# One-hot lookups of a DLRM tower: two tables in one 512-column VectorE instruction, one id buffer per pair, first loads in another order

## What is computed

```
all_vecs = concatenate([dense_proj[:, None, :], sparse_embs], axis=1)      # 2048 x 27 x 128
interactions = einsum('bnd,bmd->bnm', all_vecs, all_vecs)
z = concatenate([dense_proj, interactions[:, rows, cols]], axis=1)         # upper triangle, 351
h = maximum(concatenate([z, dense]) @ W_top1 + b_top1, 0)                  # 607 -> 512
h = maximum(h @ W_top2 + b_top2, 0)                                        # 512 -> 256
y = h @ W_top3                                                             # 256 -> 1
```

## Time and profile before

| | |
|---|---|
| median of 3 runs | 370.9 us |
| the profiled execution, whole | 370.56 us |
| its span, first to last instruction | 368.6 us |
| TensorE busy (products) | 338.4 us, 92% |
| VectorE busy | 241.6 us, 66% |
| ScalarE busy | 140.9 us, 38% |
| GpSimd busy | 245.3 us, 67% |
| DMA | 36.90 MB, mean 100 GB/s |

### The profile page before, as it was taken

How to read it: one execution, slowest core, us unless ns; L and a number is a source line. 1 busy time by engine, 2 the same in 40 slices (tenths; PEclk the granted TensorE clock), 3 DMA queues, 4 the chain that set the end, 5 groups by cost and what they waited for, 6 DMA issues and landing times.

```text
span 368.6 us, 14267 instructions
## 1 busy us (share of the span) xinstructions
PE 338.4 (92%) x6096; PEld 309.5 (84%) x6096; DVE 241.6 (66%) x702; ACT 140.9 (38%) x232; POOL 245.3 (67%) x260
## 2 busy tenths in 40 slices
PE   0686689999999999999999999999999999999797
PEld 0585589999899898989899998989999998998675
DVE  4999999998565856578565974677664884601300
ACT  2246432535143541344343441444442450447132
POOL 5777777777777777777777777777767777760000
PEclk9989999999999999999999999999999999999999
DMA  6999944332244212611243111521244112220000
GB/s 192 284 245 245 290 140 124 79 106 54 58 152 123 59 50 67 205 56 52 55 145 125 50 51 50 188 83 50 52 140 129 50 50 55 73 57 4 18 2 0
DMA packets 16567, 36.90 MB, mean 100 GB/s; under 512 B 5462, under 2 KB 8542, under 8 KB 16544
## 3 DMA queue, kind: packets, MB, share of 16 engines
q1 hardware_dynamic: 8335, 19.77, 18.0%
q0 software_dynamic: 8192, 16.79, 17.6%
q10 hardware_dynamic: 16, 0.01, 0.0%
HBM read 36.54 MB, written 0.01 MB: 99 GB/s over the span
## 4 chain that ended last, share of the span: by engine, by line
PE 85%; DVE 7%; issue 3%; DMA 3%; POOL 2%; ACT 0%; DVEq 0%
PE hid L387 14%; PE gram L413 13%; PE look_ps L341 8%; PE vec_act L314 7%; PE look_ps L343 7%; PE look_odd L341 7%; PE look_odd L343 7%; PE hid L394 7%; DVE onehot L557 5%; PE hid L341 4%; PE hid L343 4%; DMA vecs<-tbl,ids_sb 2%; DVE look_lo L565 2%; POOL vecs L297 2%; PE small L356 1%
## 5 line engine op out<-in xcount | busy, mean ns | idle before, releaser
L297 POOL DMA_INDIRECT vecs<-tbl,ids_sb x256 | 245.1, 957 | 85.1 <-issue 75.9
L557 DVE TENSOR_SCALAR onehot<-step_ids,row_no 125x256 fp32r<-125x256 int32 x640 | 199.0, 381 | 74.6 <-PE look_odd L343 35.0
L532 ACT COPY vecs_T<-vec_act 128x512 f32<-128x512 f32 x64 | 46.3, 732 | 102.2 <-PE vec_act L314 102.2
L341 PE MATMUL look_odd<-onehot,look_hi 125*128 125x256 f32 x256 | 67.3, 300 | 4.6 <-DVE look_lo L565 4.6
L341 PE MATMUL look_ps<-onehot,look_hi 125*128 125x256 f32 x256 | 67.8, 301 | 2.3 <-DVE look_lo L565 2.3
L343 PE MATMUL look_ps<-onehot,look_lo 125*128 125x256 f32 x256 | 63.7, 284 | 0.0
L343 PE MATMUL look_odd<-onehot,look_lo 125*128 125x256 f32 x256 | 62.9, 283 | 0.0
L413 PE MATMUL gram<-vecs_T 128*27 128x26 f32 x4096 | 52.8, 192 | 5.9 <-issue 3.3
L413 PEld LDWEIGHTS gram<-vecs_T 128*27 128x27 f32 x4096 | 44.1, 104 | 15.0 <-issue 9.1
L341 PEld LDWEIGHTS look_odd<-onehot,look_hi 125*128 125x128 f32 x256 | 48.8, 191 | 5.5 <-DVE look_lo L565 5.2
L341 PEld LDWEIGHTS look_ps<-onehot,look_hi 125*128 125x128 f32 x256 | 49.2, 192 | 3.2 <-DVE look_lo L565 2.7
(11 more groups left out here) (70 smaller groups left out, 282.2 us busy)
## 6 DMA issues: line engine op xcount, KB each, us to landing
step_ids<-look_ids SPq DMA_DIRECT2D x15, 640.0 KB, 4.5
raw<-tbl SPq DMA_DIRECT2D x10, 448.0 KB
vecs<-tbl,ids_sb POOLq DMA_INDIRECT x256
dense_new<-dense SPq DMA_DIRECT2D x8, 128.0 KB
dense_T<-dense SPq DMA_DIRECT2D x8, 128.0 KB, 2.9
raw<-tbl SPq DMA_DIRECT2D x10, 52.0 KB
step_ids<-look_ids SPq DMA_DIRECT2D x1, 512.0 KB
w_sb<-w SPq DMA_DIRECT2D x1, 512.0 KB
```

Source lines behind the costliest of these rows:

```text
L297: nc.gpsimd.indirect_dma_start(out=vecs[j][:, k, :], out_offset=None, in_=tables[k], in_offset=bass.IndirectOffsetOnAxis(ap=ids_sb[:, t, k ...
L341: nc.tensor.matmul(bank, look_hi[:, f, ch, :], onehot[:, i % SLOTS, c, :], start=ch == 0, stop=False)
L532: return engine_copy(vecs_T[j][:, :, lo:lo + GROUP], bank[:, :, :].rearrange("d v b -> d b v"))
L557: last = nc.vector.tensor_scalar(onehot[:, i % SLOTS, c, :], step_ids[a][0:LOOK_K, f - a * LOOKUPS // 2, :], row_no[0:LOOK_K, ch:ch + 1], ...
```

## The change

A unit becomes a quarter of a duo: 2 chunks of both tables. VectorE makes a chunk for two tables with one `tensor_scalar` of 125x512, so 2 instructions for a unit; TensorE still has 8 products of 256 columns to a unit, now alternating between the two halves of the bank. Only the first product of a bank carries `start`. A pair still has 20 units and the ring still five slots of the same size.

In the loading stage TensorE has an order of its own, `look_up_first`: all four units of a duo for its first table, then all four for its second, and only in the second round does it count `onehot_used` up. VectorE makes the first unit of a duo ahead of the last `take_low` of the duo before. The ids of a pair lie in one buffer `pair_ids`, loaded in two pieces (four tables, six tables), in pair 0 in four. The transposes of tile 0 now come after duos 0 and 1 and after duo 3.

```diff
-UNIT_CH = LOOK_CH // 2
+UNIT_CH = LOOK_CH // 4
+DUO_UNITS = LOOK_CH // UNIT_CH
+PIECES = ((0, 4), (4, LOOKUPS))
-        step_ids = [sb(f"step_ids{a}", [P, STEP_IDS, PAIR], I32) for a in range(2)]
-        onehot = sb("onehot", [LOOK_K, SLOTS, UNIT_CH, PAIR], F32R)
+        pair_ids = sb("pair_ids", [P, LOOKUPS, PAIR], I32)
+        onehot = sb("onehot", [LOOK_K, SLOTS, UNIT_CH, 2 * PAIR], F32R)
-        FIRST_TURN, SECOND_TURN = 4, 4
+        FIRST_TURN, SECOND_TURN = 2, 4
...
+                def load_ids(pair, tables, loaded):
+                    lo, hi = tables
+                    if positive(pair):
+                        sp.wait_ge(onehot_made, 2 * STEP_UNITS * (pair - 1) + hi * DUO_UNITS // 2)
...
-                load_step(0, 0, 0, slice(0, 1), first_ids_in)
+                load_ids(0, (0, 2), first_ids_in)
                 load_table(0)
-                load_step(0, 0, 0, slice(1, STEP_IDS))
                 load_table(1)
+                load_ids(0, (2, 4), pair_ids_in[0])
                 sp.dma_start(ident[:, :], identity).then_inc(ident_in, 16)
+                load_table(2)
                 load_dense_new(0)
-                load_table(2)
-                load_step(1, 1, 0)
                 load_table(3)
-                for f in range(4, LOOKUPS):
+                load_ids(0, (4, 6), middle_ids_in)
+                load_table(4)
+                load_table(5)
+                load_ids(0, (6, LOOKUPS), pair_ids_in[1])
+                for f in range(6, LOOKUPS):
                     load_table(f)
                 load_dense(0)
-                load_step(2, 0, 1)
+                load_ids(1, PIECES[0], pair_ids_in[0])
...
-                load_step(3, 1, 1)
+                load_ids(1, PIECES[1], pair_ids_in[1])
                 load_dense_new(1)
                 with sp.Fori(2, pairs) as r:
-                    load_step(2 * r, 0, r)
-                    load_step(2 * r + 1, 1, r)
+                    load_ids(r, PIECES[0], pair_ids_in[0])
+                    load_ids(r, PIECES[1], pair_ids_in[1])
...
+                def look_chunk(duo, v, part, c, slot):
+                    ch = part * UNIT_CH + c
+                    cols = slice(v * PAIR, (v + 1) * PAIR)
+                    bank = look_ps[DUO_BANK[duo]][:, cols]
+                    nc.tensor.matmul(bank, look_hi[:, 2 * duo + v, ch, :], onehot[:, slot, c, cols],
+                                     start=ch == 0 and v == 0, stop=False)
+                    return nc.tensor.matmul(bank, look_lo[:, 2 * duo + v, ch, :], onehot[:, slot, c, cols],
+                                            start=False, stop=ch == LOOK_CH - 1 and v == 1)
...
+                    for c in range(UNIT_CH):
+                        for v in range(2):
+                            last = look_chunk(duo, v, part, c, i % SLOTS)
                     last.then_inc(onehot_used, 1)
+                def look_up_first(duo):
+                    wait_for_bank(0, duo)
+                    for v in range(2):
+                        pe.wait_ge(table_split, 2 * duo + v + 1)
+                        for part in range(DUO_UNITS):
+                            n = duo * DUO_UNITS + part
+                            if v == 0:
+                                pe.wait_ge(onehot_made, n + 1)
+                            for c in range(UNIT_CH):
+                                last = look_chunk(duo, v, part, c, n % SLOTS)
+                            if v == 1:
+                                last.then_inc(onehot_used, 1)
...
+                for duo in range(DUOS):
+                    if duo == FIRST_TURN:
                         pe.wait_ge(ident_in, 16)
                         turn_half(0, 0, 0, 0)
-                for i in range(LOOKUPS):
-                    if i == SECOND_TURN:
+                    if duo == SECOND_TURN:
                         turn_half(0, 0, 0, 1)
-                    look_up(1, 1, 0, i)
+                    look_up_first(duo)
...
-                for s in range(2):
-                    for i, f, half in units(s):
-                        if i == 2 * (1 - s):
-                            dve.wait_ge(step_ids_in[s], 16)
-                        make_unit(s, s, i, f, half)
-                        if half == 1:
-                            take_low(f)
+                make_unit(0, *units(0)[0])
+                for duo in range(DUOS):
+                    for n in range(duo * DUO_UNITS + 1, (duo + 1) * DUO_UNITS):
+                        make_unit(n // STEP_UNITS, *units(n // STEP_UNITS)[n % STEP_UNITS])
+                    take_low(2 * duo)
+                    n = (duo + 1) * DUO_UNITS
+                    if duo == 0:
+                        dve.wait_ge(pair_ids_in[0], 16)
+                    if duo == 1:
+                        dve.wait_ge(middle_ids_in, 16)
+                    if duo == 2:
+                        dve.wait_ge(pair_ids_in[1], 16)
+                    if duo < DUOS - 1:
+                        make_unit(n // STEP_UNITS, *units(n // STEP_UNITS)[n % STEP_UNITS])
+                    take_low(2 * duo + 1)
...
+                for f in range(4):
+                    take_high(f)
+                take_first(0)
+                take_high(4)
+                for q in range(HALF_GROUPS):
+                    copy(0, 0, q)
+                place_dense(0, 0, 0)
+                take_high(5)
+                take_first(1)
+                take_high(6)
+                take_high(7)
+                take_first(2)
+                take_high(8)
+                take_first(3)
+                for q in range(HALF_GROUPS, GROUPS):
+                    copy(0, 0, q)
+                take_high(9)
+                take_first(4)
```

More of the change, by code:

```diff
@@ L51 @@
 SLOTS = 5
-HALF_UNITS = LOOKUPS // 2
+STEP_UNITS = LOOKUPS
+HALF_UNITS = STEP_UNITS // 2
 GATHERS = TABLES - LOOKUPS
@@ new lines, in wait_for_bank @@
+                def wait_for_bank(pair, duo):
+                    if positive(DUOS * pair + duo + 1 - DUO_BACK[duo]):
+                        pe.wait_ge(looked_up, DUOS * pair + duo + 1 - DUO_BACK[duo])
+                    if duo == 0 and positive(pair - 2):
+                        pe.wait_ge(h2_copied, pair - 1)
+                def look_chunk(duo, v, part, c, slot):
[6 more added lines that the diff above has]
+                                            start=False, stop=ch == LOOK_CH - 1 and v == 1)
@@ new lines, in look_up @@
+                def look_up(s, a, pair, i):
+                    _, duo, part = units(a)[i]
+                    pe.wait_ge(onehot_made, STEP_UNITS * s + i + 1)
+                    if part == 0:
+                        wait_for_bank(pair, duo)
+                    for c in range(UNIT_CH):
+                        for v in range(2):
+                            last = look_chunk(duo, v, part, c, i % SLOTS)
+                    last.then_inc(onehot_used, 1)
+                def look_up_first(duo):
[10 more added lines that the diff above has]
+                                last.then_inc(onehot_used, 1)
@@ L574, in unit @@
                         if look:
-                            make_unit(t + 2, j, *made[i])
-                    if look:
-                        dve.wait_ge(step_ids_in[j], 16 * (pair + 2))
+                            if j == 0 and made[i][2] == 0 and made[i][1] in (0, PIECES[1][0] // 2):
+                                dve.wait_ge(pair_ids_in[made[i][1] > 0], 16 * (pair + 2))
+                            make_unit(t + 2, *made[i])
                     for i in range(HALF_UNITS):
@@ L734, in _, with take_first @@
                 act.sem_inc(y_copied, 1)
-                ahead = LOOKUPS // 2
-                for k in range(ahead):
-                    take_high(k)
-                for s in range(2):
-                    for i, f, half in units(s):
-                        if s == 0 and i == FIRST_TURN:
-                            for q in range(HALF_GROUPS):
-                                copy(0, 0, q)
-                            place_dense(0, 0, 0)
-                        if s == 1 and i == SECOND_TURN:
-                            for q in range(HALF_GROUPS, GROUPS):
-                                copy(0, 0, q)
-                        take_looked(s, s, 0, i)
-                        if half == 1 and f + ahead < LOOKUPS:
-                            take_high(f + ahead)
+                def take_first(duo):
+                    n = (duo + 1) * DUO_UNITS - 1
+                    take_looked(n // STEP_UNITS, n // STEP_UNITS, 0, n % STEP_UNITS)
+                for f in range(4):
[16 more added lines that the diff above has]
+                take_first(4)
                 tile(0, 0, 0, first=True, mlp=False)
```

58 lines of the change are left out of this document (18 added, 40 removed).

## The result

The changed kernel takes 380.9 us (median of 4 runs; 378.26 to 384.37), the kernel before beside it 371.0 (370.31 to 371.51). The run of 384.37 us is a slow one and is left out of the ratio, which is 1.0245, 95% interval 1.0188 to 1.0302. The forecast was 374.2, with a range up to 376.2. The direction was right, but by luck: the stage that was to lose 2.5 us gained 3.4, and the loss came from work that the forecast had priced at nothing. The medians differ by 9.9 us. The profiled execution is the shortest of the four, 378.26 us with a span of 376.4 against 368.6, so the traces can explain 7.8 us.

What follows compares the result with a forecast made beforehand. The prediction took TensorE, 92% busy, as the bound, so only its end of the loading stage counted: 370.56 + 2.5 (later end of that stage) + 1.1 (one clock fall) = 374.2 us, range 370.9 to 376.2.

Steps and rivals of the forecast that it cites:

- the stage that was to lose 2.5 us: Loading stage, start of the run: TensorE was to end it at 49.05 instead of 46.56, +2.5 us.
- One-hot: 0.58 from start to start: VectorE's 512-column one-hot: 0.58 us each, a unit 1.16 instead of 1.28, 2.4 us less on VectorE in the loading stage.
- the five cases: Forecast with zero to two clock falls 0.78; gap closes 0.07; ring not binding 0.08; one-hot twice as fast 0.03; slower products or late ids 0.04.
- rival 4: Wide one-hot twice as fast, 0.32 us; TensorE ends the loading stage some 5 us earlier, 365.6 us; chance 0.03.
- The ring: Loading stage: VectorE waits for a free unit slot, losing 0.91 us a duo; a duo takes 7.93 us instead of 7.49.
- my own formula: Length of a duo in the loading stage: 2.10 + 3 x 1.16 + 1.19 + 1.16 = 7.93 us.
- the schedule: Timetable of the loading stage: VectorE starts at 6.2 instead of 5.71, TensorE is done at 49.05, +2.5 us.
- Everything behind is TensorE's own work and moves along: After the loading stage: only TensorE's end of that stage counts; later distances stay, steady part changes by at most 1 us.
- I priced POOL at nothing: GpSimd's gathers, whole run: no term in the sum; no engine but TensorE was above 67% busy.
- The clock: TensorE idle 3.5 us after tables 1 and 5 in the loading stage: one fall to half clock, +1.1 us.
- rival 2: TensorE's 1.16 us gap at 53.78 closes, hiding part of the delay: 371.4 us, or no change; chance 0.07.
- The bank halves: TensorE's products alternating between halves of a bank: cost nothing, bounds 0 and 6 us.

Runs made afterwards that it cites:

- narrow: The changed kernel with each 125x512 one-hot made by two instructions of 125x256, all else as changed: 377.5 us, ratio 1.0145 to the kernel before.

## Why the prediction missed

1. **One-hot: 0.58 from start to start was wrong, 0.41 measured.** The shortest one of 256 columns is 332 ns, of 512 columns 467: 256 more columns cost 135 ns, on top of some 0.2 us that each instruction costs. I took the slope from a subtraction of two tensors and used it against the mode table of the page "VectorE: DVE Perf Modes" of the Trainium skill. At the 0.96 GHz that this page gives, 135 ns are two columns a cycle, so the table was right about the columns: a slope and a fixed cost can't be told apart from one width. The page's row for the fixed cost divides the columns by the gain of the mode, 58 cycles + columns/gain, so it does not speak against the table, as I had it; its 58 cycles (0.06 us) are less than the 0.2 measured. And the 0.32 that I started from was itself too long: it was taken beside gathers, and 256 columns alone take 0.27 from start to start (4.29 us for 16). Of the five cases, rival 4 (0.03) was the nearest on the one-hot, though it is not twice as fast.
2. **The ring: right.** With the measured 0.41 my own formula gives 2.10 + 3 x 0.82 + 1.19 + 0.82 = 6.57 for a duo; measured 6.37, 7.02, 6.36. With dearer one-hots (narrow, 1.26 us for a unit) it was too kind: it gives 8.33, and 8.59 to 9.59 were measured. Falls of the clock are in it: TensorE is idle for 2.60 to 3.08 between duos, and after the waits of 2.80 and 3.08 its first product is 0.55 long instead of 0.38. Two waits for pieces of ids, 1.00 and 0.40, were not in the schedule.
3. **"Everything behind is TensorE's own work and moves along": this is the step that failed.** I priced POOL at nothing, since it was 67% busy. But the gathers are a chain of their own from 3 us on, one after the other, and at their tightest ran only some 2.7 us ahead of TensorE. I counted the share, not the distance. The change made some 30 gathers 0.27 longer, 8 us, and with 2.7 of room TensorE waited 8.84 us for rows, beside which its 3.4 us gain in the loading stage could not stay. I had written that behind the stage everything keeps its distances; it takes 333.3 us there (43.12 to 376.4) instead of 322.1 (46.56 to 368.6), 11.2 more.
4. **The clock: mechanism right, places not.** I priced one fall at 1.1 between duos; two falls came with waits for rows (2.03 and 3.32 us) and cost 1.7 each. None came after the idle stretches of 2.27 and 2.31 between duos.
5. **Rivals.** The gap at 53.78 did close (rival 2, 1.16 us). Rival 4 gave 365.6. With the one-hot of 0.41 and untouched gathers the kernel would have been some 3 us below the one before; that is an estimate from the 3.4 gained in the stage, and no run shows it. The bank halves cost nothing: the products follow at 0.12 in all versions.

That the gathers set the loss is shown: without the later ones, before and after are level. That the wide one-hot makes them longer is shown in the kernel (1.25 against 1.00 in the narrow one) and by itself. How much of the 10 us is the one-hot's and how much the ring's can't be split into a sum, since either delays the same chain: the new order with narrow one-hots costs 6.0 us, the wide one-hots in the loading stage take the stage 8.7 us forward against narrow and lose the same by the gathers.

## What to carry to other kernels

Before an engine is priced at nothing, look at its distance, not its share: find when its work ends and when it is needed, and what the change does to the length of each of its instructions. Where GpSimd issues indirect DMAs, every VectorE form and width that is new is a suspect for their time; measure the pair, both ways, for either engine can be the one that waits. Beside a chain of gathers that is tight, 256 columns are the better choice than 512 where the ids lie in SBUF; the price is 0.2 us of VectorE for each gather. And a one-hot made wide for the sake of VectorE is worth little where VectorE is not the bound: here 51 us less busy time on it became 10 us more of the whole.

## What was not expected of the hardware

- A gather beside back-to-back one-hots takes 0.95 us at 256 columns, 1.02 at 384, 1.15 at 448, 1.41 at 576, 1.11 at 640, 0.94 at 768, 1.02 at 1024. At 512, two of the five that ran beside them did not end until VectorE stopped (17.90 and 8.40 us). At 256 and 768 columns VectorE is the one that waits: at 256 its mean goes from 348 to 383 ns.
- Beside subtractions of two SBUF tensors a gather takes 1.97 us; a source in PSUM or a memset leave it at 0.94.
- TensorE's bursts of small products (128 of 27 by 26) take 1.30 us, and up to 2.1 while GpSimd gathers by indirect DMA, 15 us in all or 4% of the kernel before. The same traffic without a gather beside the burst leaves it at 1.30.
